# Products of two constant matrices in TensorE's waits of the first batch's chain and first filter

## The reference

```python
x  = layernorm(input)                                   # the front
u, res = split(x @ in_proj_w.T); u = silu(conv4(u))
dt, Bm, C = split(u @ x_proj_w.T); delta = softplus(dt @ dt_proj_w.T + b)
h  = scan(exp(delta * A) * h + delta * Bm * u)          # 16 states, 512 steps
y  = (h . C + u * D) * silu(res)
m  = y @ out_proj_w.T                                   # the filter
h  = layernorm(m + x)
q  = gelu(l2norm(h @ q_w.T)); k = l2norm(h @ k_w.T)
...                                                     # weighted vector, proj, fl, layernorm
h2 = gelu(h2 @ d1_w.T) @ d2_w.T + h2                    # two-layer product, layernorm
...                                                     # two picked experts, layernorm
x2 = attention(...); out = mixture(x2)                  # the second layer
```

## Time and profile before

| | |
|---|---|
| median of 3 runs | 2456.86 us |
| lowest, highest | 2449.41, 2474.56 us |
| the profiled execution | 2465.26 us |
| its span, first to last instruction | 2463.1 us |
| mean granted clock of TensorE | 0.913 |
| TensorE busy | 2051.6 us (83%) |
| VectorE busy | 1661.6 us (67%) |

### The profile page before, as it was taken

The page is one execution under the profiler, slowest core; times in us unless marked ns, Lnnn a source line. Parts: engine busy times, 40 slices in busy tenths (PEclk is TensorE's granted clock), DMA queues, the critical chain, the costliest instruction groups (busy, mean ns, idle before and its releaser), DMA issues.

```text
span 2463.1 us, 38971 instructions
## 1 busy us (share of the span) xinstructions
PE 2051.6 (83%) x11640; PEld 1426.4 (58%) x11640; DVE 1661.6 (67%) x2938; ACT 1186.9 (48%) x2703; POOL 955.0 (39%) x580
## 2 busy tenths in 40 slices
PE   4267888987899888998899888998889878888985
PEld 1043556755666556665566656665656646666664
DVE  4945886578855888558965688558876688645431
ACT  2223564345634466345643466345653456424631
POOL 1420572037710476007920287105940177203501
PEclk8577899998999899999999999999999999989997
DMA  2000012321213112321123112221123211232233
GB/s 105 0 18 0 35 51 70 115 70 41 85 65 111 57 44 69 105 99 44 57 71 115 68 48 81 78 98 62 46 74 106 87 44 60 72 125 71 71 107 119
DMA packets 82452, 175.06 MB, mean 71 GB/s; under 512 B 11448, under 2 KB 42560, under 8 KB 81984
## 3 DMA queue, kind: packets, MB, share of 16 engines
q1 hardware_dynamic: 78144, 164.05, 19.4%
q0 software_dynamic: 4096, 8.40, 1.1%
HBM read 123.71 MB, written 15.14 MB: 56 GB/s over the span
## 4 chain that ended last, share of the span: by engine, by line
PE 49%; DVE 21%; issue 14%; ACT 6%; POOL 5%; DMA 3%; SPq 1%; DVEq 1%; ACTq 0%; POOLq 0%
PE G L1064 7%; DVE HS L1555 6%; PE G L1049 5%; PE FM L1038 3%; PE G L953 3%; PE FC L1026 3%; PE G L942 3%; PE G L936 3%; DMA MW<-moe 2%; ACT REG L1349 2%; PE G L1081 2%; PE FM L906 2%; DVE maxes L1856 2%; DVE D L1550 2%; POOL Y L1984 2%
## 5 line engine op out<-in xcount | busy, mean ns | idle before, releaser
L1064 PEld LDWEIGHTS G<-REG 128*128 128x128 f32 x2560 | 347.5, 198 | 59.5 <-issue 49.7
L1555 DVE TENSOR_TENSOR_SCAN HS<-DA,D 128x1024 f32<-128x1024 f32 x128 | 359.3, 2807 | 19.4 <-ACT DA L1226 18.9
L1064 PE MATMUL G<-REG 128*128 128x64 f32 x2560 | 356.0, 272 | 3.2 <-DVE REG L1868 3.2
L1049 PE MATMUL G<-ident,REG 128*128 128x128 f32 x1280 | 241.7, 289 | 113.3 <-ACT REG L1349 111.1
L1984 POOL TENSOR_TENSOR Y<-Y,HC 128x1024 f32<-128x1024 f32 x114 | 271.1, 2378 | 163.4 <-DVE HC L1577 120.8
L1349 ACT ACTIVATE REG<-G 128x128 f32<-128x128 f32 (+3 forms) x512 | 222.9, 435 | 110.6 <-PE G L1049 105.0
L1995 POOL TENSOR_TENSOR REG<-REG,cos_t 128x512 f32<-128x512 f32 x128 | 170.8, 1334 | 257.1 <-ACT REG L1325 257.0
L1049 PEld LDWEIGHTS G<-ident,REG 128*128 128x128 f32 x1280 | 148.7, 149 | 162.1 <-issue 127.1
L1341 ACT ACTIVATE REG<-G,maxes 128x128 f32<-128x128 f32 (+3 forms) x384 | 195.4, 509 | 82.1 <-DVE maxes L1856 82.1
L1998 POOL TENSOR_TENSOR REG<-REG 128x512 f32<-128x512 f32 x128 | 207.1, 1618 | 56.9 <-DMA REG<-ROT 49.0
L1038 PE MATMUL G<-REG 64*128 64x128 f32 (+3 forms) x768 | 217.4, 482 | 9.8 <-POOL REG L1998 8.8
(11 more groups left out here) (291 smaller groups left out, 4267.1 us busy)
## 6 DMA issues: line engine op xcount, KB each, us to landing
MW<-moe SPq DMA_DIRECT2D x120, 768.0 KB, 4.2
REG<-ROT SPq DMA_DIRECT2D x256, 128.0 KB
EW<-experts SPq DMA_DIRECT2D x16, 514.5 KB, 4.6
XG<-x_rows SPq DMA_DIRECT2D x8, 960.0 KB, 5.4
y_rows<-YO SPq DMA_DIRECT2D x120, 64.0 KB, 1.5
X<-xT SPq DMA_DIRECT2D x8, 256.0 KB, 6.2
W<-weights SPq DMA_DIRECT2D x1, 2048.0 KB, 9.4
REG<-xT SPq DMA_DIRECT2D x8, 256.0 KB, 2.9
```

The costliest lines, as they stand in the source:

```text
L1049: mm = pe.transpose(G[2][:, c * P:(c + 1) * P], PR[:, n % 2, c * P:(c + 1) * P], ident[:, :])
L1064: mm = pe.matmul(G[3][:, col:col + DK], PT[:, n % 2, c * P:(c + 1) * P], V[:, c, j * P + h * DK:j * P + (h + 1) * DK], start=c == 0, stop= ...
L1555: dve.tensor_tensor_scan(HS[:, :, :].rearrange("p h s -> p (h s)"), DA[:, n % 2, :, :].rearrange("p h s -> p (h s)"), D1[:, :, :].rearrang ...
```

## The change

A helper `keep_warm(n)` issues n products of `avg` and `ones`, 128 columns each, into G[0]; nothing reads them and they raise no semaphore. In `front` the twelve steps get 16, 6, 8, 3, 6, 2, 2, 2, 4, 3, 4 and 4 of them, ahead of the step's waits, 60 in sum. In a phase 1 without token work, every filter step (30 of them) gets two, ahead of its waits, also 60. Nothing else moves.

```diff
@@ tensor engine
             pe.wait_ge(s_made, 4)
+            WARM_FRONT, WARM_SLOT = (16, 6, 8, 3, 6, 2, 2, 2, 4, 3, 4, 4), 2
+
+            def keep_warm(n):
+
+                for _ in range(n):
+                    pe.matmul(G[0][:, 0:P], avg[:, :], ones[:, :], start=True, stop=True)
...
+            def filter_step_warm(b, k, f):
+                keep_warm(WARM_SLOT)
+                filter_step(b, k, f)
+
             def phase_1(b, t, f):
-                each_step(b, t, f, filter_step, token_use, front_start, attention_end, early_scan)
+                each_step(b, t, f, filter_step if t is not None else filter_step_warm, token_use, front_start, attention_end, early_scan)
...
             def front(b):
                 for p in range(12):
+                    keep_warm(WARM_FRONT[p])
                     if p == 2:
                         pe.wait_ge(s_first, n_first)
```

## The result

The changed kernel is slower: 2475.05 us against 2463.8 us, medians of 22 runs each taken together; the ratio is 1.0047 with a 95% interval of 1.0026 to 1.0067. A second measurement of the same two kernels gave 1.0061 (1.0033 to 1.0088). By the ratios the loss is 12 and 15 us. The forecast was +1.1 us, 2458 us in a range of 2447 to 2471, worked out from the 2456.86 us that three runs of the kernel before had given; over 22 runs that kernel itself came out 7 us higher.

The account below looks back on a forecast made before the run. Front and first filter were taken as chains of small handovers, TensorE often the engine waited for, partly at half clock. Front 5.3 - 4.2 + 0.4 = +1.5, filter -0.4: +1.1 on 2456.86, so 2458 us, range 2447 to 2471.

Parts of the forecast that it names:

- four cases: The forecast (0.55) and three alternatives in front and first filter, from -13 to +13 us around the median.
- The sixteen: Products ahead of the front's first mean: nothing hides them, clock rises within them, cost 5.3 us.
- What comes back in the front: Mean, variance, spread and first convolution run faster at full clock: 4.2 of 5.1 us, counting one fall of the clock.
- the six products: Ahead of the front's second convolution: need 1.3 us in an idle time of 0.84, so +0.4 us.
- The filter: First filter, 137.8 to 260.1 us: cost 4.3 less gain 4.7, -0.4 us, between -13.2 and +4.6.
- The price: Two added products cost 0.43 us at full clock, 0.86 at half; eight pairs on the filter's gapless chain cost 4.3 us.
- three stretches counted as saved: Filter half clock: first (144.1 to 150.9 us), third (185.0 to 188.4), fourth's front half (from 205.5); 1.7 + 1.4 + 1.6 us.
- The second: Filter's half-clock stretch 161.1 to 171.4 us, holding about 4.0 us; no saving counted.
- the last: Filter's half-clock stretch 236.2 to 260.1 us, holding 6.3 us; no saving counted.
- Rival 1: Clock held up nearly throughout the filter: -13.1 us, 2444 us; chance 0.12.
- Rival 2: Filter's half-clock stretches stay where they are and the gapless chain's eight pairs are paid: +6.1 us, 2463; chance 0.25.
- Rival 3: Front's sixteen products do not raise the clock before the first convolution: +13.4 us, 2470; chance 0.08.

Follow-up runs that it names:

- scan_sixty: Kernel before plus 60 products in the first scan, four behind each of the first 15 C products, none in the front's chain or filter; 1.0048 (1.0012 to 1.0085).
- filter_only: Changed kernel with only the filter's 60 products, none in the front; against the kernel before 1.0009 (0.998 to 1.0037).
- front_only: Changed kernel with only the front's 60 products, no pairs in the filter; against the kernel before 1.0029 (0.9998 to 1.0061).
- before_again: The kernel before, unchanged, timed again against itself as a measure of scatter; 0.9994 (0.9957 to 1.0032).
- the cut kernels: Kernels before and changed, cut off behind the first filter (256.83 against 258.13 us) or behind the first attention (419.21 against 417.05 us).

## Why the prediction was wrong

**The step that failed** is in its first paragraph: "The change adds work only ahead of 260.1 us", "So two stretches can react", and with it the bound of the range, four cases that all end at the filter. The sum put all time behind 260 us at nothing. The products act there without running there: 120 more of them lengthen the program past two steps at which the experts' loads of all batches slow down, by 0.28 us in all. TensorE waited for these loads 21 times before, and its waits grew by 4.8 us (28.9 to 33.7) and in the second pair of profiles by 6.3 (28.6 to 34.9).

That 60 products which delay nothing up to the filter cost the whole kernel time was shown (scan_sixty, 12 us by its ratio, between 3 and 21); that they do so through the loads was not, since no run changed the loads and not the length, and filter_only, with loads as long, came out at 1.0009 (0.998 to 1.0037), which is compatible with a cost of 5 to 9 us but not with 12.

Taken from the rows, the loads' waits and the local loss of 1.3 to 1.9 us make 6 to 8 of the 12 to 15 us measured. The rest goes with more half clock behind the waits: in the means of the fifteen traces, waits and clock together, the filters of batches 1 to 6 are 3.0 us longer, the last one is 0.9 us shorter (108.8 against 109.6 us), the closing stretch is 3.6 us longer, and the attention stages of batches 1 to 5 are, each against its own kind, 0.4 and 0.6 us longer (159.9 against 159.5 us, 166.4 against 165.8). That is about 8 us behind the first filter and some 10 with the local loss. In the runs of scan_sixty and front_only, half clock sums to 449 and 453 us in the means of 12, against 421 and 430 us in the kernel before beside them; but twelve other runs of that kernel (before_again) had 434, so a part of this is scatter. That the slow loads bring this half clock about is not shown, since no run changed one without the other.

**The number** was off for a second reason, the base. The +1.1 us were put on the median of three runs, 2456.86 us. On the 2463.8 us of 22 runs the same forecast gives 2464.9, and a range as wide, 2454 to 2478, would have held the 2475 measured. That would have been luck: the change moved the time by 12 us, not by 1.

**The sum up to the filter's end** held: +1.1 forecast, 1.3 to 1.9 on the cut kernels, 3.0 in the one pair of profiles, of which a part is scatter.

- The sixteen: forecast 5.3 us, measured 6.1 (mean at 13.89 instead of 7.83) and in front_only 5.0. The clock rose 5.4 us after their start, later than the 2.8 to 4.7 us that the two rises of before had suggested, and 3.1 us after it in front_only.
- What comes back in the front: forecast 4.2, with one fall of the clock. One fall came, at 19.9 us, in the place named. From the filter's start, 2.15 us late, 6.1 + 0.4 - 2.15 = 4.35 us came back (0.4 as forecast for the six products). In front_only the filter starts 1.1 us late.
- The filter: forecast -0.4, measured +0.9 in the one pair of profiles and -0.6 in the means of five executions with pairs and eleven without, whose scatter is 2 to 5 us. The price was right (0.45 us a pair at full clock in the gapless chain). Of the three stretches counted as saved, the fourth's saving is borne out in every execution, the first was only displaced, and the third went, as it does at times without pairs. The second, written off, lost a third, and the last lost 3.5 of its 23.9 us.
- Rival 1 (the clock held up) did not come: half clock in the filter fell from 53.9 to 37.7 us only. Rival 2's idea that the stretches stay was wrong for the fourth.
- Rival 3 did not come: the convolution ran at full clock, 3.67 us.

**The rule weighed against the change**, that of the Trainium skill ("TensorE: Matmul & The Clock Gate", section "Why this matters for your kernels") by which long idle gaps between bursts make the clock drop, was rightly distrusted: in the changed kernel, too, the clock fell at 19.9 us with no idle time over 1.65 us since 7.68, and pairs put into the filter's short gaps cut its half clock from 48.6 to 67.5 us (eleven executions) to 32.1 to 40.4 (five).

**The range** ended at 2471, with the highest of four cases none of which reached past the filter, and the median came out at 2475. Of the 11 us that the two medians lie apart, some may belong to scatter, which has a source that the earlier trace rows did not show. The attention stages come in the main in two kinds, here two of the kernel before taken again (stretch, length, TensorE busy, granted clock):

```profile
256.30:423.70 167.40, 144.30 (x850) 0.91 0.14 48
547.50:706.90 159.40, 135.91 (x853) 0.97 0.17 56
```

The same work takes 159.4 us with 10.2 us at half clock, and 166 to 167 with 24 to 30. A run has eight of them, and which ones are long differs from run to run.

## What to carry to other kernels

Filler work on TensorE is bought twice: each product delays the real one behind it by its own length wherever the queue has no gap, and 16 of them in front of a ready operand cost 5.0 to 6.1 us here, of which the whole front with its 60 brought back 4.3 to 4.4. Put them only behind a wait that is longer than they are, and expect little: here 20 us less half clock in the filter bought no time that could be told from scatter. Read a clock's stretches from several executions, since the same kernel places them differently. And instructions that are off every path can still cost: when a long kernel changes by some tenths of a per cent after code was added, look at its DMA loads from first to last packet, and run the same number of instructions where they delay nothing, before blaming the place.

## What the runs showed of the hardware that was not expected

- A 768 KB load of the experts' weights takes 2.84 to 2.88 us from first to last packet in six executions with 0 to 35 added products, 3.04 to 3.07 us in five with 45 or 60, and 3.12 to 3.14 us in four with 104 or 120, though no transfer was changed. The median packet takes 234 ns in all of them; the last packets start later.
- Half clock of 10 or 24 us in one attention stage, from identical work, makes 6.5 us of difference; over 35 runs of the kernel before, time and half-clock time (twice the time, times one less the mean granted clock) go together with a correlation of 0.94 and a slope of 0.45 us per us.
- The loads' step does not come from code fetched at the same time: loads without a code packet beside them show it too (2.82 to 2.87 against 3.01 to 3.12 us).
- One more input array of 32 KB, which nothing reads, changed neither the time nor these loads.
